# Attention loop of a two-layer graph network: the last group's sums in three pieces on TensorE, the edge counts behind the next queries

## What is computed

```
scores = jnp.sum(Q_t * K_s, axis=-1) * scale + (edge_features @ We + be)   # 8 heads per edge
max_s = jax.ops.segment_max(scores, targets)                               # per target node
exp_s = jnp.exp(scores - max_s[targets])
denom = jax.ops.segment_sum(exp_s, targets) + 1e-10
aggregated = segment_sum(exp_s / denom[targets] * V_s, targets)
x = x + aggregated @ Wo + bo
```

## Time and profile before

| | us |
|---|---|
| median of 3 runs (lowest to highest) | 1144.46 (1143.58 to 1145.53) |
| the profiled execution, its own time | 1143.35 |
| span of that execution, first to last instruction | 1141.3 |
| TensorE busy (matmul) | 874.7 |
| VectorE busy | 735.2 |
| GpSimd busy | 605.4 |

### The profile page before, as it was taken

The page is one execution under the profiler, slowest core; times in us unless marked ns, Lnnn a source line. Parts: engine busy times, 40 slices in busy tenths (PEclk is TensorE's granted clock), DMA queues, the critical chain, the costliest instruction groups (busy, mean ns, idle before and its releaser), DMA issues.

```text
span 1141.3 us, 19921 instructions
## 1 busy us (share of the span) xinstructions
PE 874.7 (77%) x4796; PEld 740.3 (65%) x4796; DVE 735.2 (64%) x2605; ACT 375.4 (33%) x1062; POOL 605.4 (53%) x597
## 2 busy tenths in 40 slices
PE   5338988888878978978878977944787878888774
PEld 3127877777777867867767867833575666656654
DVE  8626667667667667666666666659766476574763
ACT  4603233233233233233233233206253433424430
POOL 0355667566666656666666656400554555545552
PEclk9756676676676676676676676667798998989988
DMA  5882354343353444353353353210211211212211
GB/s 162 193 167 61 109 141 113 105 137 109 107 139 110 111 123 122 109 140 103 112 138 111 109 140 108 79 65 13 86 51 41 52 48 47 52 41 51 51 45 38
DMA packets 103350, 109.51 MB, mean 96 GB/s; under 512 B 36803, under 2 KB 81807, under 8 KB 103311
## 3 DMA queue, kind: packets, MB, share of 16 engines
q0 software_dynamic: 25600, 66.10, 21.8%
q1 hardware_dynamic: 77719, 43.07, 14.2%
HBM read 97.94 MB, written 11.16 MB: 96 GB/s over the span
## 4 chain that ended last, share of the span: by engine, by line
issue 35%; PE 29%; SPq 15%; DVE 11%; DMA 6%; another core or an unknown queue 3%; DVEq 1%; ACT 0%
PE ps_q L1714 13%; SPq L556 5%; PE ps_c L1698 4%; PE ps_r L1733 3%; DMA qwin<-q_tab 3%; PE ps_f L1777 2%; PE ps_f L1778 2%; PE ps_c L1694 1%; SPq L694 1%; SPq L686 1%; PE ps_f L1758 1%; SPq L687 1%; DVE sc L1055 1%; SPq L699 1%
## 5 line engine op out<-in xcount | busy, mean ns | idle before, releaser
L758 POOL DMA_INDIRECT kv<-kv_tab,idx x416 | 434.7, 1045 | 297.0 <-issue 118.5
L797 POOL DMA_INDIRECT kv<-hs_tab,idx x176 | 170.4, 968 | 219.5 <-DMA hs_tab<-qkv 72.5
L1714 PE MATMUL ps_q<-qwin,ST 128*128 128x128 f32 x832 | 213.2, 439 | 44.7 <-DMA qwin<-q_tab 20.8
L1536 ACT ACTIVATE S<-iota,nloc 128x128 f32<-128x128 f32 x384 | 122.1, 389 | 368.7 <-remote 319.7
L1714 PEld LDWEIGHTS ps_q<-qwin,ST 128*128 128x128 f32 x832 | 186.2, 329 | 49.5 <-issue 38.8
L1049 DVE TENSOR_TENSOR prod<-kv,ps_q 128x512 f32<-128x512 f32 (+1 forms) x128 | 74.2, 580 | 146.2 <-PE ps_q L1714 111.8
L1733 PE MATMUL ps_r<-wv,S 128*128 128x137 f32 x832 | 145.6, 344 | 0.0
L1733 PEld LDWEIGHTS ps_r<-wv,S 128*128 128x128 f32 x832 | 143.7, 255 | 0.4
L1863 PE MATMUL ps_r<-qkv,xt 128*128 128x128 f32 x800 | 98.5, 280 | 25.6 <-ACT xt L1624 14.9
L1863 PEld LDWEIGHTS ps_r<-qkv,xt 128*128 128x128 f32 x800 | 93.6, 194 | 29.8 <-ACT xt L1624 15.1
L1698 PEld LDWEIGHTS ps_c<-we,attr_s 128*128 128x128 f32 (+1 forms) x256 | 63.0, 321 | 26.4 <-DMA attr_s<-in_attr 18.6
(11 more groups left out here) (262 smaller groups left out, 1257.4 us busy)
## 6 DMA issues: line engine op xcount, KB each, us to landing
dloc_b<-dloc_tab SPq DMA_DIRECT2D x32, 416.0 KB
kv<-kv_tab,idx POOLq DMA_INDIRECT x416
attr_s<-in_attr SPq DMA_DIRECT2D x32, 192.0 KB
kv<-hs_tab,idx POOLq DMA_INDIRECT x176
kv_tab<-qkv SPq DMA_DIRECT2D x4, 640.0 KB, 3.4
x_tab<-x SPq DMA_DIRECT2D x32, 64.5 KB
qwin<-q_tab SPq DMA_DIRECT2D x32, 64.0 KB
xwin<-in_x SPq DMA_DIRECT2D x32, 64.0 KB
```

Source lines behind the costliest of these rows:

```text
L758: pool.indirect_dma_start(out=kv[:, b, t, :], out_offset=None, in_=kv_tab, in_offset=bass.IndirectOffsetOnAxis(ap=idx[:, b, t:t + 1], axis ...
L797: pool.indirect_dma_start(out=kv[:, j, t, 0:D], out_offset=None, in_=hs_tab, in_offset=bass.IndirectOffsetOnAxis(ap=idx[:, j, t:t + 1], ax ...
L1536: A.activation(S[:, b, t, :], iota[:], ACT.Abs, bias=nloc[:, g, t:t + 1] if known(g) else nloc[:, bass.ds(g, 1), t:t + 1].rearrange("p g t ...
L1714: mm = M.matmul(ps_q[c % 2][:, (t - t0) * D:(t - t0 + 1) * D], ST[:, b, t, :], qwin[:, b, :], start=True, stop=True)
```

## The change

In a step, TensorE now runs the last group's sums as three pieces (`SUMS`: tiles 0 to 6, 7 to 9, 10 to 12), one ahead of each of the first three turns, and the carry's two matmuls behind the third turn. The 13 counts move from between the second and third turn to behind chunk 0 of the next group's queries. VectorE's `carry` moves from ahead of `backward` to behind `scan_partitions_back`, and `add_sums` behind `shifted`. The number and the shapes of the instructions stay the same.

```diff
-TV = T - 2
+SUMS = [(0, 7), (7, 10), (10, T)]
...
                 if edges:
                     scan_partitions(g, b, A)
+                    backward(g, b, A)
+                    if far:
+                        set_idx(g + 2, b, s_idx)
+                    scan_partitions_back(g, b, A)
                 if nodes:
                     carry(g - 1, 1 - b, B)
                 if edges:
-                    backward(g, b, A)
+                    shifted(g, b, A)
                 if nodes:
                     add_sums(g - 1, 1 - b, B)
-                if edges:
-                    if far:
-                        set_idx(g + 2, b, s_idx)
-                    scan_partitions_back(g, b, A)
-                    shifted(g, b, A)
-                if nodes:
                     average(g - 1, 1 - b, B)
...
             def step(g, b, edges=True, nodes=True, more=True):
                 if edges:
                     query(g, b, (2, 3))
                 if nodes:
-                    window_sums(g - 1, 1 - b, edges)
-                elif edges:
+                    window_sums(g - 1, 1 - b, 0)
+                if edges:
                     turned_front(g)
+                if nodes:
+                    window_sums(g - 1, 1 - b, 1)
                 if edges:
                     wait_apart(pe, s_cf, g + 1, (s_part, 1))
                     M.transpose(p_c1, c1[:, b, 0:P], ident[0:H, 0:H]).then_inc(s_cfT, 1)
...
+                if nodes:
+                    window_sums(g - 1, 1 - b, 2)
+                if edges:
                     pe.wait_ge(s_v2, g + 1)
                     M.transpose(p_v2, bx[:, :, 0], ident[:]).then_inc(s_v2T, 1)
+                if nodes:
+                    window_carry(g - 1, 1 - b, edges)
+                if edges:
                     wait_apart(pe, s_cb, g + 1, (s_part, 1))
                     M.transpose(p_c2, c2[:, 1:P + 1], ident[0:H, 0:H]).then_inc(s_cbT, 1)
                 if edges and more:
                     query(g + 1, 1 - b, (0,))
+                if edges:
+                    counts_of(g, b)
                 if nodes:
                     pe.wait_ge(s_agn, g)
                     M.transpose(ps_f[:, 0:D], agn[:], ident[:]).then_inc(s_agTp, 1)
```

More of the change, by code:

```diff
@@ L1721, in turned_front, with window_sums, window_carry @@
                 M.transpose(p_v1, f1[:, :, T - 1], ident[:]).then_inc(s_v1T, 1)
-            def window_sums(g, b, edges=True):
-                pe.wait_ge(s_wv, 2 * g + 1)
-                pe.wait_ge(s_Sa, (NCH - 1) * (g + 1))
-                pe.wait_ge(s_S, 2 * g + 2)
-                for t in range(T):
+            def window_sums(g, b, part):
+                for t in range(*SUMS[part]):
+                    if t == 0:
+                        pe.wait_ge(s_wv, 2 * g + 1)
+                        pe.wait_ge(s_Sa, (NCH - 1) * (g + 1))
+                        pe.wait_ge(s_S, 2 * g + 2)
                     if t == TB:
                         pe.wait_ge(s_wv, 2 * g + 2)
-                    if edges and t == TV:
-                        turned_front(g + 1)
                     mm = M.matmul(ps_r[:, 0:C + 1], S[:, b, t, :], wv[:, t, :], start=(t == 0), stop=(t == T - 1))
-                mm.then_inc(s_agg, 1)
+                    if t == T - 1:
+                        mm.then_inc(s_agg, 1)
+            def window_carry(g, b, edges=True):
                 if not (known(g) and g == 0):
@@ L1741, in window_sums, with counts_of @@
                 M.matmul(p_fb, isf[:], facd[:], start=True, stop=True).then_inc(s_rc, 1)
+            def counts_of(g, b):
+                pe.wait_ge(s_oh, 2 * g + 2)
+                if not (known(g) and g == 0):
+                    pe.wait_ge(s_od, g)
+                for t in range(T):
+                    mm = M.matmul(ps_f[0:HI, 3 * D:3 * D + LO], oh_hi[:, b, :, t], oh_lo[:, b, :, t],
+                                  start=(t == 0), stop=(t == T - 1))
+                mm.then_inc(s_hist, 1)
             def step(g, b, edges=True, nodes=True, more=True):
@@ L1752, in step @@
                     M.transpose(p_c1, c1[:, b, 0:P], ident[0:H, 0:H]).then_inc(s_cfT, 1)
-                    pe.wait_ge(s_oh, 2 * g + 2)
-                    if not (known(g) and g == 0):
-                        pe.wait_ge(s_od, g)
-                    for t in range(T):
-                        mm = M.matmul(ps_f[0:HI, 3 * D:3 * D + LO], oh_hi[:, b, :, t], oh_lo[:, b, :, t],
-                                      start=(t == 0), stop=(t == T - 1))
-                    mm.then_inc(s_hist, 1)
+                if nodes:
+                    window_sums(g - 1, 1 - b, 2)
+                if edges:
                     pe.wait_ge(s_v2, g + 1)
                     M.transpose(p_v2, bx[:, :, 0], ident[:]).then_inc(s_v2T, 1)
+                if nodes:
+                    window_carry(g - 1, 1 - b, edges)
+                if edges:
                     wait_apart(pe, s_cb, g + 1, (s_part, 1))
```

## The result

The changed kernel took 1229.26 us (median of 4 runs, 1225.94 to 1230.65), the kernel before 1144.02 (1141.98 to 1145.53) on the same chip: a ratio of 1.0748, 95% interval 1.0719 to 1.0777. That is slower, as forecast, but 40 us above the forecast of 1189 and outside its range. The profiled execution took 1225.94 us. One warning for all that follows: the kernel before took 1144, 1166 and 1168 us on some chips and 1051 on another, so only a ratio against the kernel before on the same chip carries.

What follows compares the result with a forecast made beforehand. TensorE's query run plus the chain to the `qwin` load was taken to bound each step. Counts added 31 times 1.56 = 48.4 us, less 3 for the ends, +45 on 1143.35: 1188.4, forecast 1189 us, range 1171 to 1203.

Steps and rivals of the forecast that it cites:

- The query run: TensorE from chunk 0 to the end of chunk 3, 10.48 us without idle; counts there add 1.56 us a step.
- The spacing by the Trainium skill: Counts at 53 ns each, about 0.7 us a block, a time near 1165 us; not used for the sum.
- The clock: TensorE's granted clock in the queries: expected to stay at 0.50, the level of 1.2 GHz.
- rival C: Clock stays at 2.4 GHz through the queries, run 4.8 us less; 1117 us with half the steps; chance 0.08.
- The pieces of sums: Sums in three pieces between turns: 0.7 to 1.4 us a piece of three tiles, covered by waits there.
- the scan chain: Scans and four turns from the queries' end to next chunk 0: 0.5 to 1.0 us shorter, worth nothing.
- Against: nothing in the list depends on what moved: Argument against SyncE's list getting through faster, which would let the scans and turns decide; priced 1153 us, chance 0.09.
- the load chain: VectorE's chunk 2, old rows, SyncE's list, `qwin` load, chunk 0: 10.15 us, decides when chunk 0 starts.
- hangs on chunk 2 and not on any turn: SyncE's list before the `qwin` load: follows chunk 2, so shorter scans and turns gain nothing.
- a sign of being wrong: SyncE's list much shorter or longer than 5.2 us would show the forecast wrong.
- Rival D: Turns become the later chain, missed by 1.49 us in half the steps: 23 us more, 1212 us; chance 0.04.

Runs made afterwards that it cites:

- counts_only: The kernel before with only the 13 counts moved behind chunk 0 of the next queries: ratio 1.0381, 45.8 us over 1166.2.
- before_again: The kernel before, unchanged, run once more for its profile on a chip with hold-ups: ratio 1.0004.
- queries_first: The kernel before with the load of `qwin` at the head of SyncE's list: 0.9439 without hold-ups, 0.9954 on a chip with them.
- pace_counts_back: The changed kernel with tile 8's gather waiting for the fourth turn and the counts back between second and third turn: 0.9964, chip without hold-ups.
- before_pace_fourth: The kernel before with tile 8's gather waiting for the fourth turn instead of the second: 0.9957, chip without hold-ups.
- The two kernels of the last batch: The kernel before with tile 4's gather waiting for the fourth turn: 1.0482; the same with the load of `qwin` first as well: 1.0379.
- gathers_on_small: The kernel before, tile 8's gather waiting for the first turn only, 1 of 13 `dloc_b` tiles loaded from group 3: 0.9803, again 1.0370.

## Why the prediction was wrong, point by point

- **The query run**, and that nothing in it hides the counts, was right. It grew in the step shown by 1.92 us, over all steps by 1.77 (11.97 less 10.20). Forecast were 1.56, at most 1.67. A record costs what was forecast, 0.12 us (1.78 less a tail of 0.30, over 12). But from the first record to L1782 it is 354.38 less 352.67, 1.71 us; the rest lies at the seams. From chunk 0 to the counts it is 2.00 us, from chunk 0 to L1769 before it was 1.86 (344.84 less 342.98). This term was mis-sized by 0.2 to 0.4 us a step, some 6 to 11 us. That `counts_only` measured 46 us, next to the forecast's 45, is luck. Beside `before_again`, on another chip at 1166 us, its run is longer by 2.05 us a step (12.22 less 10.17), 64 us in 31 steps, and its chunk 0 comes 0.54 us sooner behind the first turn (7.24, 7.78), 17 us. The forecast had neither of the two.
- **The spacing by the Trainium skill** ("TensorE: Matmul & The Clock Gate", section "Back-to-back issue gap") of N / 1.2, 53 ns for 64 columns, was rightly not used: the row gives 0.12 us a record, and `counts_only` +46 us where that rule would have given 21.
- **The clock** did as forecast, no rival C. Smaller holes did not hold it up in `queries_first` either: there no hole in steps 3 to 29 is over 0.72 us, and the granted clock over the query runs was still 0.50 to 0.59. The window of the changed kernel over the query run (busy us of PE, PEld, DVE, ACT, POOL, granted clock, DMA share, GB/s):

```profile
350.00:363.00 13.00, 12.33 (x55) 10.99 (x56) 7.23 (x17) 3.27 (x10) 7.07 (x6) 0.50 0.20 61
```

- **The pieces of sums** show no cost on the chip without hold-ups: `pace_counts_back` (0.9964) is within noise of `before_pace_fourth` (0.9957). But no run shows the scan chain 0.5 to 1.0 us shorter either, as the forecast had it. With the gathers paused the changed order has its fourth turn at 4.30 to 4.47 us, and the old order without hold-ups at 3.98.
- **The step that failed** is "Against: nothing in the list depends on what moved", and with it that the load chain "hangs on chunk 2 and not on any turn". SyncE's list waits on no turn, but GpSimd's gather of tile 8 does, and it moved from 3.79 us behind the first turn (340.42 less 336.63) to 2.25 (368.83 less 366.58). On a chip with hold-ups, that one earlier release makes one row of seven gathers, beside which SyncE's later issues and the result of TensorE's third turn come late. The list grew from 6.03 to 8.37 us, which the forecast itself had named as a sign of being wrong, and the fourth turn moved from 5.81 to 7.06. Chunk 0 comes 1.59 us later behind the first turn; with 1.77 of the query run, less 0.22 between the last query and the first turn, this is 3.14 of the 3.15 us by which the step grew.
- **Rival D** came nearest in price, and not by its mechanism. The turns did come late, by 4.1 us in 23 steps where I had priced a miss at 1.49 us in half of them, but they did not become the later chain: the load chain stayed it in most steps (chunk 0 still 1.64 us behind the fourth turn in the mean). The late results had no rival of their own, because I had seen "remote" waits of 1 us at the turns and asked only what they cost, not what ends them.

What is shown: that the release of tile 8's gather is one cause (done alone in the kernel before it costs 45 us, 1210.7 less 1166.2; put off in the changed kernel it gives back 58 of 87), and that the counts are the other (46 us alone). What stays open: by which path a gather holds up SyncE's instructions and a result of TensorE on its way to VectorE, whether it is the gather's issuing or its own data (only the bytes of a plain load were varied), why the new order of TensorE spares the first turn and not the third, and why one chip does not do it. The two kernels of the last batch were to settle whether the overlap itself is the cause and did so only in part, since a row of gathers stayed in the way. `before_pace_fourth` and `pace_counts_back` were not run on a chip with hold-ups, so how much of the 58 us the kernel before would gain as well is open, and whether the pieces of sums alone, with the gathers paused, would beat the kernel before there; on the other chip it stands at 0.9964.

## What to carry to other kernels

Before moving an instruction, list every engine that waits for its semaphore, GpSimd's gathers too, and ask what starts sooner; a wait that only paces another engine can be worth more than the work that is moved. A load that the next step waits for belongs at the head of its queue: `queries_first`, one load moved to the head of its list, is faster than the kernel before on both kinds of chip, by 5.6 and by half a per cent (0.9439 and 0.9954). And a kernel with such waits is to be timed on more than one chip: `gathers_on_small` read 0.980 on one and 1.037 on another. The changed kernel itself was never timed on the chip without hold-ups.

## What the runs showed of the hardware

- The kernel before took 1051 us in one batch and 1144 to 1168 in the five other sets of runs. There is no trace of the kernel before from the chip without hold-ups; `before_pace_fourth` (1046 us there) stands in for it. Its list took 4.44 us, against 6.0 to 6.8 for the kernel before on two other chips, and its fourth turn came at 3.98 us, against 5.8 to 6.4. The loop is not all of the difference: between the spans of `before_again` and `before_pace_fourth` lie 122 us, of them 53 from the first to the last first turn, 12 ahead of it and 57 behind it. What is slower in those last two parts was not looked into.
- A gather's row in the trace is not the whole of it. GpSimd shows 0.95 us each, 1.25 apart, yet the late turns came 3.0 us behind a gather's start in the middle (the pattern above). The Trainium skill, "Perfetto Trace Analysis", section "DMA Instruction — SWDGE (GPSIMD)", says that such a row ends when the descriptors are written and not when the data has moved; these rows agree with it: in the changed kernel the last gather's row ended at 372.29, and the gathers' queue still moved 0.13 MB from 373.00 to 373.70.
- At the end of that hold-up in the changed kernel the DMA engines themselves had little to do: here are the windows between the last gather's end and the load of `qwin`, and over that load.

```profile
372.40:373.00 0.60, 0.00 (x0) 0.00 (x0) 0.00 (x0) 0.52 (x2) 0.00 (x0) 1.00 0.08 27
373.00:374.00 1.00, 0.00 (x0) 0.00 (x0) 0.09 (x1) 0.97 (x4) 0.00 (x0) 0.50 0.70 197
```

- SyncE's rows in the loop are 0.33 to 0.52 us long on the chip without hold-ups. On the others they go from under 0.01 us (373.73 above is a short one) to 0.7 us and more. A short row can be written after its load has begun: of the traffic in the second window most is the gathers' (0.13 MB), but from 373.00 to 373.70 the queue of SyncE's loads moved 66 packets, 0.03 MB, all ahead of the row at 373.73, and from 372.30 to 373.00 none.
